# Decoder layer on one core: expert addresses sent by a 512-byte transfer instead of through TensorE, and the down blocks' copies shared out anew

## The reference, cut to what matters

```python
def kmoe(x_flat, W_router, A, B, scale, bias, ...):      # up: 32x32 -> 64x64, down: 64x64 -> 32x32
    logits = x_flat @ W_router.T                         # 64 experts
    vals, idx = jax.lax.top_k(logits, 2)
    probs = softmax(vals)
    Y = einsum('nkoi,nij,nkpj->nkop', A[idx], xs, B[idx])
    out = einsum('nkop,nk->nop', Y, probs)
    return out * scale + bias
x = x + kmoe_down(gelu(kmoe_up(layernorm(x))))
```

## Time and profile before

| | |
|---|---|
| time, median of 3 runs | 1346.06 us (1343.82 to 1347.63) |
| profiled execution, its own time | 1348.9 us |
| span in its trace | 1347.1 us |
| TensorE matmuls busy | 1216.1 us (90%) |
| VectorE busy | 957.9 us (71%) |
| ScalarE busy | 1077.5 us (80%) |
| GpSimd busy | 596.6 us (44%) |
| DMA mean | 32 GB/s |

### The profile page before, as it was taken

How to read it: one execution, slowest core, us unless ns; L and a number is a source line. 1 busy time by engine, 2 the same in 40 slices (tenths; PEclk the granted TensorE clock), 3 DMA queues, 4 the chain that set the end, 5 groups by cost and what they waited for, 6 DMA issues and landing times.

```text
span 1347.1 us, 51835 instructions
## 1 busy us (share of the span) xinstructions
PE 1216.1 (90%) x16466; PEld 974.0 (72%) x16466; DVE 957.9 (71%) x3651; ACT 1077.5 (80%) x3126; POOL 596.6 (44%) x1870
## 2 busy tenths in 40 slices
PE   6799999999999999999999999999999999987534
PEld 5667687877777787777778787777778787765423
DVE  1365779695968879695978779596878879594514
ACT  2456899898988899898989899798989889887441
POOL 3122446362645446363645546263545536252513
PEclk9999999999999999999999999999999999998555
DMA  9200101010100101010010101010010101010000
GB/s 290 42 17 10 33 15 42 12 42 18 35 25 17 36 17 42 12 40 20 27 33 16 37 15 41 14 39 21 19 42 10 42 12 41 8 30 15 25 18 9
DMA packets 67745, 43.09 MB, mean 32 GB/s; under 512 B 18577, under 2 KB 66322, under 8 KB 67218
## 3 DMA queue, kind: packets, MB, share of 16 engines
q1 hardware_dynamic: 67474, 39.77, 10.6%
HBM read 35.51 MB, written 4.19 MB: 29 GB/s over the span
## 4 chain that ended last, share of the span: by engine, by line
PE 54%; DVE 16%; SPq 10%; issue 10%; ACT 3%; DMA 2%; POOL 2%; DVEq 1%; POOLq 1%; ACTq 0%
SPq L419 9%; PE P L738 5%; PE X L796 4%; PE P L706 4%; PE PT L761 4%; PE P L717 4%; PE PT L796 4%; PE P L695 3%; DVE own L1061 3%; PE F L875 3%; PE X L783 3%; PE F L900 3%; DVE chosen_dn L360 3%; PE S L754 3%; PE G L835 2%
## 5 line engine op out<-in xcount | busy, mean ns | idle before, releaser
L360 POOL COPY chosen_dn<-experts 64x64 f32 x1024 | 224.5, 275 | 225.7 <-issue 160.4
L598 ACT ACTIVATE probs<-probs,neg_max 128x128 f32<-128x128 f32 (+1 forms) x512 | 226.4, 444 | 24.3 <-DVE neg_max L1020 20.7
L346 POOL COPY chosen_up<-experts 32x128 f32 x512 | 182.4, 356 | 105.6 <-POOL chosen_up L346 51.2
L346 ACT COPY chosen_up<-experts 32x128 f32 x512 | 151.3, 296 | 25.1 <-PE G L881 11.2
L1020 DVE CUSTOM_DVE_ANT_0 probs<-S,distance 128x128 f32<-128x128 f32 (+1 forms) x512 | 151.8, 350 | 13.8 <-PE S L754 10.3
L761 PE MATMUL PT<-ident,probs 128*128 128x128 f32 x768 | 136.2, 287 | 10.1 <-DVE probs L1038 5.7
L637 ACT ACTIVATE hT<-h 64x1024 f32<-64x1024 f32 x64 | 126.7, 1980 | 15.3 <-DVE h L1151 13.9
L1038 DVE TENSOR_TENSOR probs<-probs,rinv 128x768 f32<-128x768 f32 x128 | 128.7, 1006 | 4.4
L875 PE MATMUL F<-chosen_up,own 64*64 64x64 f32 x2048 | 91.1, 230 | 38.6 <-DMA chosen_up<-in_experts_up 25.9
L875 PEld LDWEIGHTS F<-chosen_up,own 64*64 64x64 f32 x2048 | 76.9, 141 | 66.7 <-issue 55.1
L706 PE MATMUL P<-ctxT,wk 128*128 128x256 f32 x512 | 122.1, 382 | 2.1 <-DVE x L998 2.1
(11 more groups left out here) (130 smaller groups left out, 2858.4 us busy)
## 6 DMA issues: line engine op xcount, KB each, us to landing
chosen_up<-in_experts_up SPq DMA_DIRECT2D x1024, 16.0 KB, 1.6
x<-in_x SPq DMA_DIRECT2D x16, 256.0 KB, 2.7
ctxT<-in_ctxT SPq DMA_DIRECT2D x16, 256.0 KB, 3.1
out<-x2b SPq DMA_DIRECT2D x16, 256.0 KB, 2.3
experts<-in_experts_up SPq DMA_DIRECT2D x2, 1024.0 KB, 19.9
wk<-in_xWk SPq DMA_DIRECT2D x1, 1024.0 KB
wo<-in_xWo SPq DMA_DIRECT2D x1, 1024.0 KB
wv<-in_xWv SPq DMA_DIRECT2D x1, 1024.0 KB, 7.7
```

What stands on the lines that cost most here:

```text
L346: last = copy(to[row:row + D1, n * 2 * F1:(n + 1) * 2 * F1], experts_up[k][:, bass.ds(held[g % loaded(units), unit], 2 * F1)])
L360: last = copy(dst, src.rearrange("p (m c) -> p m c", m=2))
L598: act.activation(probs[:, e % 4, lo:hi], probs[:, e % 4, lo:hi], ACT.Exp, bias=neg_max[:, e % 4, rt:rt + 1], scale=-1.0, accum_out=rsum[:, ...
```

## The change: what it does

Four things change together.

1. The addresses no longer go through TensorE. `place` becomes an integer tile, and a new step `send_dn` / `send_up` on SyncE moves its 64 rows of two numbers into the one row `offsets` by a DMA. It stands right behind top_dn and top_up in the list.
2. The diagonal form has the probabilities alone: one VectorE instruction instead of two, and the matmul of route_spreading has 128 columns instead of 256. The three casts are gone from keep_up and from keep_dn.
3. `offsets` now lies in token order. The engines' loads read it through strided views; for the down layer a load covers only one half of a group's blocks.
4. Of a down group's 16 blocks GpSimd copies ten (6 to 15), ScalarE two (4, 5), VectorE four as before. With ten blocks GpSimd holds the addresses of two groups instead of four.

```diff
-            "pool": {"up": range(4, 6), "dn": range(8, 16)},
+            "pool": {"up": range(4, 6), "dn": range(6, 16)},
             "dve": {"up": range(0), "dn": range(0, 4)},
-            "act": {"up": range(6, 8), "dn": range(4, 8)}}
+            "act": {"up": range(6, 8), "dn": range(4, 6)}}
...
-logits_dn.1@3 logits_dn.2@3 logits_dn.3@3 part@3 fold@3 ln1 top_dn@3 gap_dn@3 weights_dn@3 ln3_turn@2 q.0@1 q.1@1
+logits_dn.1@3 logits_dn.2@3 logits_dn.3@3 part@3 fold@3 ln1 top_dn@3 send_dn@3 gap_dn@3 weights_dn@3 ln3_turn@2 q.0@1
...
         def loaded(units):
 
-            return min(4, HELD // len(units))
+            return 4 if 4 * len(units) <= HELD else 2
...
+            if layer == "up":
+                of = offsets[0][:, :].rearrange("p (g u) -> p g u", g=UP_GROUPS)
+                pieces = [(of[:, g:g + ahead, units.start:units.stop], range(g, g + ahead), units)]
+            else:
+                each, pieces = DN_TOK // 2 * TOPK, []
+                of = offsets[1][:, :].rearrange("p (e j i u) -> p e i j u", e=2, j=2, u=each)
+                for half in range(2):
+                    some = range(max(units.start, half * each), min(units.stop, (half + 1) * each))
+                    for i in range(g // 2, (g + ahead) // 2):
+                        if some:
+                            pieces.append((of[:, half, i, :, some.start - half * each:some.stop - half * each], (2 * i, 2 * i + 1), some))
...
-                eng.wait_ge(offsets_ready[layer], c + 1)
+                eng.wait_ge(offsets_ready[layer], at(c, 16, 16))
...
+            def send(c, layer):
+
+                groups = (UP_GROUPS, DN_GROUPS)[layer]
+                sp.wait_ge(route_step[layer], at(c, 4, 1))
+                for name in choosers_of(("up", "dn")[layer]):
+                    if name != "sync":
+                        after(sp, chosen[name][layer], at(c, groups, 0))
+                to = offsets[layer][:, :].rearrange("p (n k) -> p n k", k=TOPK)
+                sp.dma_start(to, place[layer][:, :]).then_inc(offsets_ready[layer], 16)
...
-                pe.wait_ge(route_ready[layer], at(c, 2, 2))
-                pe.matmul(G[:, 128:384], route_ones[:, :], route_diag[layer][:, :], start=True, stop=True).then_inc(route_spread[layer], 1)
+                pe.wait_ge(route_ready[layer], c + 1)
+                pe.matmul(G[:, 128:256], route_ones[:, :], route_diag[layer][:, :], start=True, stop=True).then_inc(route_spread[layer], 1)
...
+                after(dve, offsets_ready[layer], at(c, 16, 0))
                 dve.tensor_scalar(place[layer][:, :], top_idx[layer][:, 0:TOPK], float(step), None, ALU.mult)\
```

More of the change, by code:

```diff
@@ L3 @@
+import itertools
 import math
@@ L77 @@
 x2.0@2 x2.1@2 ln3_stats@2 k_keep.3@1 ln3_root@2 ln1_stats ln1_root ln3@2 xnT2@1 router_dn@3 logits_dn.0@3
-logits_dn.1@3 logits_dn.2@3 logits_dn.3@3 part@3 fold@3 ln1 top_dn@3 gap_dn@3 weights_dn@3 ln3_turn@2 q.0@1 q.1@1
[L79 to L86, removed]
+logits_dn.1@3 logits_dn.2@3 logits_dn.3@3 part@3 fold@3 ln1 top_dn@3 send_dn@3 gap_dn@3 weights_dn@3 ln3_turn@2 q.0@1
+q.1@1 q_keep.0@1 spread_dn@3 keep_dn@3 score.0@1 ln3_keep@2 mask.0@1 choose_dve.16@3 q_keep.1@1 logits_up@2
+choose_act.16@3 top_up@2 send_up@2 choose_pool.16@3 choose_pool.17@3 choose_pool.18@3 choose_pool.19@3 q.2@1 q.3@1
+choose_dve.17@3 exp.0@1 scale.0@1 gap_up@2 q_keep.2@1 turn1 choose_dve.18@3 weights_up@2 turn_a.0@1 choose_act.17@3
+score.1@1 q_keep.3@1 catch_a.0@1 dn_first.0@3 turn_b.0@1 mask.1@1 choose_act.18@3 choose_act.19@3 spread_up@2 v.0@1
+dn_weigh.0@3 keep_up@2 choose_sync.0@2 xnT1 dn_second.0@3 exp.1@1 catch_b.0@1 choose_dve.19@3 score.2@1 dn_first.1@3
+v_keep.0@1 scale.1@1 pv.0@1 y_keep.0@3 mask.2@1 dn_weigh.1@3 choose_sync.1@2 choose_sync.2@2 choose_act.0@2
+choose_sync.3@2 choose_pool.20@3 choose_act.20@3 choose_act.21@3 choose_act.1@2 turn_a.1@1 choose_dve.20@3 f.0
+dn_second.1@3 choose_act.2@2 score.3@1 exp.2@1 choose_act.3@2 choose_dve.21@3 choose_pool.21@3 dn_first.2@3 y_keep.1@3
 choose_dve.22@3 scale.2@1 dn_weigh.2@3 catch_a.1@1 f_keep.0 keep_out.0@1 choose_pool.22@3 choose_act.4@2
@@ L330, in fetch_offsets @@
                 return
[L331 to L337, removed]
+            if layer == "up":
[9 more added lines that the diff above has]
+                            pieces.append((of[:, half, i, :, some.start - half * each:some.stop - half * each], (2 * i, 2 * i + 1), some))
+            for view, groups, some in pieces:
+                values = nc.values_load_multi_w_load_instructions(
+                    view, engines=[kind], min_val=0, max_val=(EXPERTS - 1) * step,
+                    skip_runtime_bounds_check_because="an index of one of 64 logits times the table's step")[1]
+                for (group, unit), value in zip(itertools.product(groups, some), values):
+                    held[group % ahead, unit] = value
         def choose_up(copy, held, g, units):
@@ L412, in choose @@
                 v, half = divmod(g, 2)
[L413 removed]
+                sp.wait_ge(offsets_ready[0], at(c, 16, 16))
                 fetch_offsets(at_sp, mybir.EngineType.SP, g, "sync")
@@ L1092, in weights @@
                 eye = spread(ident[0:F1, 0:TOKENS], 2, TOPK)
[L1093 to L1096, removed]
+                dve.tensor_tensor(route_diag[layer][0:F1, :].rearrange("p (n k) -> p n k", k=TOPK), eye,
+                                  spread(prob[layer][:, :], 1, TOKENS), ALU.mult).then_inc(route_ready[layer], 1)
             def keep_up(c):
                 dve.wait_ge(route_spread[0], c + 1)
[L1101 to L1106, removed]
                 for n in range(2 * TOPK):
```

22 lines of the change are left out of this document (5 added, 17 removed).

## The result

The changed kernel takes 1406.31 us, median of 4 runs (1401.31 to 1408.31), against 1346.63 us before: ratio 1.0432, 95% interval 1.0413 to 1.0451 (this ratio is an estimate over the runs; the two medians alone give 1.0443, and the ratios below can differ from those of the medians as little). It is slower by 60 us, far outside the range forecast. The profiled execution took 1401.31 us, the shortest of the four and 52.4 more than that of before.

A forecast was written before the change was run, and what follows sets the result against it. TensorE, busy 90% of the span, was taken as the bound. 14 turns x 0.4 us gained (-5.6), +2.5 last turn, +0.2 the one before: -2.9 on 1348.9, so 1346.0 us; own range 1340 to 1346, whole range 1335 to 1351.

The forecast's parts named there:

- the spreading matmuls: Two a turn on TensorE; half the columns were to take 0.22 us off each 0.43 us.
- what reaches turn_a.0: Down layer, ahead of turn_a.0: its input was to arrive 0.2 us sooner, between 0.1 and 0.5.
- the transfer: SyncE's new DMA of addresses was to land 1.6 to 2.7 us after issue.
- GpSimd's loads took 0.565 us for 8 addresses and 2.03 for 32: GpSimd's register loads: 4 and 16 addresses of a down pair were to take 0.32 + 1.05 = 1.37 us.
- this stretch: From the store to up.7, where SyncE issues 32 transfers in 20 us: untouched by the change, it would only slide along.
- the margin: GpSimd in a steady turn: 1.0 us later with its up blocks, covered by a 4.40 us wait, so no cost.
- the last turns: GpSimd's down groups, lacking cover: dn_first.3 2.5 us late in the last turn, 0.2 more for the one before.
- The third: Rival: GpSimd becomes the bound and is slower, its copies and VectorE's hindering each other; 2.2 us a turn, 1380 us; chance 0.15.
- a floor of about 600 ns for a register load: GpSimd's loads of 4 addresses: some 0.28 us more a pair, 1.1 us in the last turn, sum -1.8 instead of -2.9.
- The port lock: VectorE and GpSimd share a port pair, locked for a whole instruction; a group's 2.33 us against 1.48 agreed in kind.

The follow-up runs named there:

- e4: The changed kernel, with each load taking the aligned whole runs of four addresses that hold the wanted ones, on all engines: 1352.24 us, ratio 1.0023.
- e13: e4 with the old shares (GpSimd 8, VectorE 4, ScalarE 4) of the down groups in the last two turns alone: 1340.92 us, ratio 0.9932.
- e9: The changed kernel without its transfer: table made by the wide spreading matmul and one VectorE copy a layer, in token order: 1459.31 us, ratio 1.0814.
- e1: The kernel before, with GpSimd copying ten of a down group's blocks, ScalarE two, and packed loads for two groups: 1359.47 us, ratio 1.0074.
- e10: The changed kernel with loads in whole runs of four for the up layer alone, on every engine: 1364.67 us, ratio 1.0118.
- e5: The changed kernel with loads in whole runs of four on GpSimd alone: 1359.17 us, ratio 1.0070.
- e11: The changed kernel with loads in whole runs of four for the down layer alone, on every engine: 1376.15 us, ratio 1.0189.
- e6: The changed kernel with loads in whole runs of four on ScalarE alone: 1411.84 us, ratio 1.0464.
- e12: e2 with an idle memset of 1060 columns on GpSimd ahead of each down group: 1381.42 us, ratio 1.0248.
- e2: The changed kernel with the old shares of the down groups (GpSimd 8, VectorE 4, ScalarE 4): 1352.22 us, ratio 1.0018.

## Why the prediction was wrong, point by point

**Right: the spreading matmuls.** "I take half: 0.22 us off." The chain of work in the change:

```profile
577.30 0.22 PE G L869 x2
```

It is 0.22 where it was 0.43. The gain is there in e4 and e13, whose turns are 0.34 and 0.41 us shorter than before; forecast were 0.4, between 0.3 and 0.7. These two kernels also change other things, so the 0.41 isn't shown to be this gain alone.

**Right: what reaches turn_a.0 and the transfer.** The wait ahead of turn_a.0 stayed (4.1 us in 11 times). The transfer's issue and landing:

```profile
L422 SPq DMA_DIRECT2D offsets<-place x32: 463/498/507, 115.2 to 1362.3; - x32
...
DMA to landing us min/median/max: 1.6/1.7/2.7
```

1.6 to 2.7 had been taken from the earlier trace rows. That the transfer is worth keeping where GpSimd has no slack is shown by e9.

**Wrong, and the step that failed: "GpSimd's loads took 0.565 us for 8 addresses and 2.03 for 32, so 0.061 an address and 0.075 a load; 4 and 16 addresses make 0.32 + 1.05".** The 16 took 1.09; the 4, which lie in two runs of two, took 0.98. Worse, the sum has no term for the loads of the up layer at all. They keep their number and their eight addresses, so they were taken as unchanged, and each went from 0.565 to 1.88 us. The prediction had even set this stretch aside, "The change touches nothing in it, so it only slides along", and it is there, ahead of up.5, that TensorE now waits. The rows of before held packed loads alone, and the price per address was carried over to a view with another stride. Part 3 of the change, the layout, had been read as a matter of how many loads there are. It would have been worth bounding from both sides like the spreading matmul: nothing in the earlier trace rows said that a strided load costs the same.

**Wrong: the margin.** "GpSimd then is 1.0 us later than now with its up blocks; a wait of 4.40 us further on takes that up." The 4.40 were not all: 11.0 us of slack were there, and the change used 12.4. Of these the forecast had 4 x (1.37 - 1.02) = 1.4 for the down loads (measured 4.2), 3.0 for the copies (measured 1.7, and 1.5 in other steps) and 0 for the up loads (5.2). With the forecast's 4.4 us the cover would have held, as e1 shows with some 4 (turns of 76.48) and e4 with some 8 (75.94). The line isn't sharp: e10, with some 9.3 us more on GpSimd, had turns of (1218.25 - 292.08)/12 = 77.2 us in its profiled execution. That one was 9 us longer than the other four, though, and its turns are of two kinds: eight of 76.4 in the mean and four of 78.1 to 79.3, three of these with a lower clock. The line is why the parts cost +0.7% and +0.2% alone and +4.3% together. That GpSimd's total is the cause is shown from three sides: less work on it (e4, e5, e10, e11), the same work with ScalarE relieved (e6), later addresses (e9). e12 agrees, with VectorE's part in it open. What a microsecond beyond the line costs isn't settled: the budget gives 1.4 of the 2.8 us in the turn read, and TensorE's lower clock, for which the forecast had no term, is in nine turns of twelve.

**Wrong in size: the last turns.** "2.5 us late, 1.9 to 3.1", and 0.2 for the turn before. The change lost 5.8 us in the last turn (73.91 against 68.11) and 5.6 in the one before (76.07 against 70.48). With the loads mended (e4) it is 3.8 and 2.8. The last turn's four pairs were put at 20.2 us from the first copy to the end of the last; they took 23.5 in the change (1366.36 to 1389.82) and 22.2 in e4. The turn before had been looked at least: dn_first's longest wait for GpSimd in it was 3.3 us before and is 5.0 in e4. e13 shows that the shares in these two turns are the cause of what e4 loses there, since nothing else differs from e4.

**The rivals.** The third came true in its result, "GpSimd becomes the bound", with a chance of 0.15 and a mechanism that wasn't the one: it priced a copy at 0.28 us of GpSimd's time and drew the line at 0.254, and they took 0.20 (256.7 us for 1280), before 0.22 (224.5 for 1024); its 2.33 us for a group of eight as a rule didn't appear. The wait also was not where it had been looked for. dn_first waits 2.9 us in ten turns, `up` 31.7: GpSimd delivers the down blocks nearly in time, and is late with what it does after them.

**The two rules cited.** The Trainium skill, page DMA: Bandwidth & Descriptors, section Latency and other measured facts, gives a floor of about 600 ns for a register load. I used it for the four addresses and added 0.28 us, as an estimate. The shortest loads here, 0.54 us on ScalarE and 0.56 on GpSimd before, lie a little under that floor; but the four addresses took 0.98, so as a price the floor was too low by 0.4 us, and the measurements decide. The port lock of the Trainium skill's page SBUF — State Buffer, section SBUF: two separate sides, cited behind the third rival, agrees in kind with groups like the one at 1313.12 in the change, whose ten copies took 2.80 us where others took 1.95. It isn't what set this result, since GpSimd's down copies took less time each than before (0.20 against 0.22 us).

## What to carry to other kernels

When data that an engine's sequencer reads changes its layout, price each load by the runs of its view and not by its count, also where the number of loads and addresses stays; if the trace has only packed loads, the strided price is an unknown and needs both bounds. For an engine off the critical path, add up all its waits in a turn and set them against all its added work, loads and earlier or later inputs included: parts that each fit can together cross the line, and beyond it the cost comes in every turn. If the bottleneck's waits grow long, look at its granted clock too, as work that is unchanged can take longer. A share that does no harm in steady turns can be wrong in the last ones; choosing it by turn was worth 0.9 points here, from 1.0023 to 0.9932.

## What the runs showed of the hardware

A TENSOR_LOAD of addresses in runs of two took 0.97 us for 4 and 1.88 for 8 on GpSimd, so some 0.23 us an address. In runs of four or more it took 0.59 for 8 and 1.08 for 16, and in one run 0.565 for 8 and 2.03 for 32, some 0.06 an address. On ScalarE eight took 1.80 us in pairs and 0.55 packed. Loading twice as many addresses, half of them unwanted, was 0.8 us faster. On VectorE eight in runs of four took 0.62 and 16 in one run 1.10. Runs of three, or of two with another spacing, weren't tried, so where between two and four the step lies is open.

A transfer of 64 rows of 8 bytes within SBUF landed 1.7 us after its issue in the median of 32.

TensorE's granted clock was at its lower level, 0.50, for the 5.7 us that follow the change's wait of 3.17 us, and the mean clock of the steady turns was 0.98 in the change and 0.96 in e9, whose waits for `up` reach 3.2 us, against 1.00 before, where the longest was 2.0.

Memsets of 128 x 1060 on GpSimd, eight a turn, came with VectorE's down copies taking 85.9 us instead of 59.3 in twelve turns (e12 and e2).
